# An early-fusion layer in one kernel: the mask of the transposed scores moves into spare rows of the shift product, the image comes on 96 partitions, the sink values lie in PSUM

## The chip, the cores and the metric

The kernel runs on one core of a Trainium2 chip. The metric is the device time of one execution in microseconds (us). The profile is of one execution; its span runs from the first to the last recorded instruction.

## The reference, cut to what matters

64 images of 12 x 224 x 224 become 196 tokens each, 32 text tokens join them (T = 228), then come an attention layer with 12 heads of 16 and a mixture of 8 experts. Everything is fp32.

```python
pooled = x.reshape(Bb, Cc, n, K, n, K).sum(axis=(3, 5))     # 16 x 16 patches, n = 14
h = jnp.einsum('bcij,ce->bije', pooled, channel_weights)    # 12 channels -> 192
h = concat([h, txt]); xn = layernorm(h)
...
att = jnp.einsum('bhqd,bhkd->bhqk', rope(q), rope(k)) * scale
att = jnp.where(causal, att, -inf)
att = softmax(concat([sink, att]))[..., 1:]                 # one sink value per head
h = h + ((att @ v) @ W_proj + b_proj) * rezero
h = h + moe(layernorm(h))                                   # top 2 of 8 experts
```

## The kernel before, in words

The first pass is a software pipeline over the 64 images. One step works on five images at once: p (loaded, pooled, channels summed), a (first norm, q, k and v, rotation, turns), m (scores and their row maxima), t (scores again, transposed, with the maximum taken off, then exp and attend) and z (projection, second norm, gate, slots). Every engine runs its own list of these pieces in an order written by hand (step_tensor, step_scalar, step_vector, pass1_gpsimd), and semaphores join the lists. The second pass runs the experts over the scattered rows; nothing in it is edited.

The order of TensorE in a step, with S for score_t, C for score and T for turn_qk: S0 C0, project, S1 C1 S2 C2, turn_xn, S3, attend 0, make_qk 0, C3 S4, turn_xf, make_qk 1, C4 S5, gate_logits, C5 S6, attend 1, S7 C6, rank, S8 C7 C8, attend 2, T0 T1 T2, turn_shift, make_v, turn_y, T3 T4 T5, sum_channels, turn_yn. S2, S5 and S8 are the ones that treat the second half of the keys for four heads; the other six S treat the first half (and the sink row) for two heads.

The pieces that the change and the prediction touch:

- The image. load_image (L406) is one transfer: 112 partitions (4 channels of a group x 14 patch rows x 2 halves) times 3 groups, each piece 8 image rows in one run. fold_image (L686, GpSimd) adds the two halves of a group, 896 elements; pool_image (L502, VectorE) sums it to 14 values; spread_patches (L694, GpSimd) multiplies them with a 0/1 table so that each patch row stands in its own columns; sum_channels (L844, TensorE) multiplies by the channel weights, three groups for each of two halves of the tokens.
- The transposed scores. score_t (L953 to L964) adds three products in PSUM: k times q, `sel` times shift_t (takes off the row maximum), and the identity times mask_k (the causal mask, L956 and L959). shift_t has 128 rows of which 26 are in use.
- The shift. max_scores (L571, VectorE) leaves the row maxima in `top`; make_shift (L578) takes the larger of `top` and the sink value; turn_shift (L939, TensorE) turns it, waiting also for `routed`, which assign sets (`slot`, L675); round_shift (L795, ScalarE) rounds it to the high part; split_shift (L586, VectorE) makes the low part and shift_ready, on which S0 of the next step and turn_xf wait.
- The rotation. rotate (L533, L535, VectorE) reads make_qk's result, add_rotation (L719, GpSimd) adds, high_parts (L747, ScalarE) and low_parts (L726, GpSimd) split q and k into pieces for turn_qk (L906). exp_gap (L833, ScalarE) waits for choose (L620, VectorE), exps are L805 and L808; place_q is L548, copy_y L814, weigh L644 to L657, place_k L559, normalize L593 to L598, turn_yn L1003, copy_yn L820, norm2_apply L770 (it waits for scattered rows, L1284).

VectorE's order in the middle of a step is: rotate 0, max 3, pool_image 1, rotate 1, max 4, max 5, choose, max 6, pool_image 2, max 7, max 8, make_shift, assign, place_k 1, split_shift, weigh, place_k 3, normalize, place_k 5. GpSimd's is: first statistics, fold 0, second statistics, fold 1, add_rotation 0, fold 2, add_rotation 1, low_parts 0 and 1, spread_patches, scatters.

## Time and profile before

| | |
|---|---|
| median of 3 runs | 2945.84 us (2934.99 to 2946.96) |
| the profiled execution | 2942.38 us, of which the span is 2940.6 us |
| TensorE, busy share of the span | 95% |
| GpSimd / VectorE / ScalarE, busy share | 69% / 70% / 58% |
| mean granted TensorE clock | 0.983 of full speed |
| first pass / second pass | until about 1730 us / the rest |

The shares of busy time are means over both passes. Matmuls are pipelined and the records show each with its latency, so a busy TensorE isn't one at its peak; the spacing of starts tells what one matmul costs. A wait in brackets at a row of the timeline is the idle time of the engine in front of it, with the instruction that ended it.

### The profile page before, as it was taken

The numbers are of one execution on the slowest core, as the hardware profiler recorded it, in microseconds if no ns is written. First come the engines' busy times: TensorE is split into PE (matmuls) and PEld (weight loads), VectorE is DVE, ScalarE is ACT, GpSimd is POOL, SyncE is SP. The second block draws the span as 40 slices with busy tenths as digits, with TensorE's granted clock in tenths as the row PEclk, the third lists the DMA queues.
The fourth block names the chain that finished last, engine by engine and source line by source line (L and its number), as shares of the span: only waits on it lengthen the run. The fifth ranks groups of instructions, "written<-read, shape, count | busy, mean of one in ns | idle before, by whom it ended". The sixth has DMA issues, their size and how long they took to land. (4 is left out here: it accounts for less than half of the span.)

```text
span 2940.6 us, 65980 instructions
## 1 busy us (share of the span) xinstructions
PE 2788.6 (95%) x21712; PEld 2515.0 (86%) x21712; DVE 2049.6 (70%) x5657; ACT 1692.5 (58%) x4074; POOL 2022.5 (69%) x2070
## 2 busy tenths in 40 slices
PE   2899999999999999999999976999999999999998
PEld 1788888888888888888888866999999989999997
DVE  3577777777777777777777745767676767676766
ACT  1466666666665666666566644655565656565655
POOL 3578888888888888788888733655566555565655
PEclk9899999999999999999999988999999999999999
DMA  6455455544443444444344222333333333323242
GB/s 191 141 176 175 167 165 173 156 122 122 115 107 106 119 121 122 119 111 111 107 121 121 56 48 61 56 60 51 63 55 65 49 65 49 65 45 65 46 68 43
DMA packets 206006, 292.47 MB, mean 99 GB/s; under 512 B 95670, under 2 KB 167675, under 8 KB 205874
## 3 DMA queue, kind: packets, MB, share of 16 engines
q1 hardware_dynamic: 82642, 241.41, 28.2%
q0 software_dynamic: 122880, 47.00, 11.4%
q10 hardware_dynamic: 352, 2.41, 0.3%
q8 instruction: 69, 1.13, 0.2%
q14 instruction: 63, 0.52, 0.1%
HBM read 201.73 MB, written 93.90 MB: 101 GB/s over the span
## 5 line engine op out<-in xcount | busy, mean ns | idle before, releaser
L1493 POOL DMA_INDIRECT out<-arena,who x320 | 595.3, 1860 | 291.4 <-DVE who L1372 180.5
L571 DVE TENSOR_REDUCE top<-bank 114x2 f32<-114x456 f32 (+1 forms) x576 | 352.8, 622 | 87.3 <-PE bank L930 71.1
L686 POOL TENSOR_TENSOR arena<-arena 112x896 f32<-112x896 f32 x192 | 403.0, 2100 | 13.2 <-DMA arena<-in_x 13.2
L1466 PE MATMUL bank<-w_dn,hid 128*114 128x192 f32 x3840 | 401.9, 264 | 0.0
L1466 PEld LDWEIGHTS bank<-w_dn,hid 128*114 128x114 f32 x3840 | 390.3, 180 | 0.0
L1439 ACT ACTIVATE arena<-bank 128x456 f32<-128x456 f32 x320 | 176.3, 551 | 342.1 <-PE bank L1430 332.2
L1284 POOL DMA_INDIRECT moe_rows<-row,slot x256 | 294.4, 1150 | 103.9 <-issue 85.0
L548 ACT ACTIVATE pieces<-bank 64x456 fp32r<-64x456 f32 x384 | 209.4, 545 | 147.1 <-PE bank L906 144.9
L1443 DVE TENSOR_TENSOR arena<-bank,arena 128x456 f32<-128x456 f32 x320 | 201.5, 630 | 96.6 <-ACT arena L1439 84.6
L726 POOL TENSOR_TENSOR qk<-rot_c,qk 114x384 fp32r<-114x384 f32 x256 | 253.8, 1013 | 19.0 <-ACT qk L747 19.0
L1426 PE MATMUL bank<-pieces 128*128 128x456 f32 x640 | 241.2, 377 | 21.9 <-DVE arena L1443 15.2
L805 ACT ACTIVATE prob<-bank 115x456 f32<-115x456 f32 x384 | 208.0, 542 | 78.0 <-PE bank L956 77.3
L1430 PE MATMUL bank<-pieces 128*128 128x456 f32 x640 | 238.5, 373 | 0.0
L1455 DVE TENSOR_TENSOR hid<-arena,hid 128x456 fp32r<-128x456 f32 x320 | 201.6, 630 | 52.3 <-ACT hid L1450 34.3
L1429 PE MATMUL bank<-pieces 128*128 128x456 f32 x640 | 237.9, 372 | 0.0
L1450 ACT ACTIVATE hid<-arena 128x456 fp32r<-128x456 f32 x320 | 186.9, 584 | 88.1 <-DVE arena L1443 86.7
L1428 PE MATMUL bank<-pieces 128*128 128x456 f32 x640 | 237.5, 371 | 0.0
L1427 PE MATMUL bank<-pieces 128*128 128x456 f32 x640 | 236.8, 370 | 0.0
L1483 POOL TENSOR_TENSOR rms<-rms,minus_half 114x4 f32<-114x4 f32 x82 | 85.4, 1042 | 193.5 <-DVE rms L1364 193.5
L906 PE MATMUL bank<-ident_r,qk 114*128 114x114 f32 x1536 | 202.1, 282 | 10.7 <-POOL qk L726 10.7
L502 DVE TENSOR_REDUCE pooled<-arena 112x14 f32<-112x896 f32 x192 | 206.5, 1076 | 6.4 <-POOL arena L686 6.4
L906 PEld LDWEIGHTS bank<-ident_r,qk 114*128 114x128 f32 x1536 | 186.5, 196 | 23.0 <-POOL qk L726 23.0
(171 smaller groups left out, 7216.3 us busy)
## 6 DMA issues: line engine op xcount, KB each, us to landing
arena<-in_x SPq DMA_DIRECT2D x63, 2352.0 KB, 11.8
arena<-moe_rows SPq DMA_DIRECT2D x82, 363.4 KB
moe_rows<-filler SPq DMA_DIRECT2D x20, 1453.5 KB
out<-h SPq DMA_DIRECT2D x64, 171.0 KB
out<-arena,who POOLq DMA_INDIRECT x320, 5.0
arena<-in_w_t SPq DMA_DIRECT2D x9, 512.0 KB
arena<-in_w_t SPq DMA_DIRECT2D x18, 256.0 KB
moe_rows<-row,slot POOLq DMA_INDIRECT x256, 7.3
```

The lines of the kernel that those rows point to most:

```text
L571: nc.vector.tensor_reduce(dst, src, AX.X, ALU.max).then_inc(maxed[k], 1)
L686: nc.gpsimd.tensor_tensor(xin[at.par][:, g, 0:mid], xin[at.par][:, g, 0:mid], xin[at.par][:, g, mid:XF], ALU.add).then_inc(x_folded, 1)
L726: ins = nc.gpsimd.tensor_tensor(lo, of, first.bitcast(fp32), ALU.subtract)
L906: ins = nc.tensor.matmul(dst[:, TT * (2 * pair + half):TT * (2 * pair + half + 1)], src, ident_r[0:TT, 0:TT], start=True, stop=True)
L1284: nc.gpsimd.indirect_dma_start(out=moe_rows[0:SLOTS, :], out_offset=bass.IndirectOffsetOnAxis(ap=slot[at.par][:, 2 * t + k:2 * t + k + 1], ...
L1426: nc.tensor.matmul(dst, hi[:, 0, col], za_hi[:, :], start=True, stop=False)
L1427: nc.tensor.matmul(dst, hi[:, 0, col], za_lo[:, :], start=False, stop=False)
L1428: nc.tensor.matmul(dst, lo[:, 0, col], za_hi[:, :], start=False, stop=False)
L1429: nc.tensor.matmul(dst, hi[:, 1, col], zb[:, :], start=False, stop=False)
L1430: ins = nc.tensor.matmul(dst, lo[:, 1, col], zb[:, :], start=False, stop=True)
L1466: ins = nc.tensor.matmul(dst, hid2[:, j, h_part, at], w_dn2[e_par][:, j, w_part, :], start=(j == 0 and s % 2 == 0 and part == 0), stop=(j ...
L1493: nc.gpsimd.indirect_dma_start(out=out[:, :], out_offset=bass.IndirectOffsetOnAxis(ap=who[par][:, s:s + 1], axis=0), in_=ys[par][:, s, :], ...
```

## The change

Three parts. The mask of the transposed scores goes into rows 14 to 127 of shift_t, which are written once (`low`), and `sel` gets the identity in these rows, so that the product that takes off the maximum adds the mask as well. For that the heads are taken in two groups of six: the shift has 14 rows (TOP) per group and is turned in four pieces instead of two. The image comes on 96 partitions (8 row pairs x 12 channels) in eight transfers with runs of 448 elements; it is folded and pooled in three bands of 5, 5 and 4 patch rows, the spread is left out, and sum_channels is one product for each half of the tokens. The sink values of make_shift lie in PSUM columns. In the lists of VectorE and GpSimd some pieces change place.

```diff
-XP = GRP * SIDE * 2
-XF = HALF * IMG
+XP = CH * HALF
+XF = 2 * IMG
+BANDS = ((0, 5), (5, 10), (10, SIDE))
+NG = len(BANDS)
+TOP = 2 * PAIRS + 2
...
-        sel[h, h] = -1
-        sel[HEADS + h, h] = -1
+        sel[h % PAIRS, h] = -1
+        sel[PAIRS + h % PAIRS, h] = -1
+        sel[TOP + q, h, q] = 1
+    low = np.zeros((128, 3, TT), f)
+    low[TOP:, 0] = low[TOP:, 2] = later.T
...
+        sink_top = bank[7][0:TT, 480:480 + 2 * HEADS].rearrange("p (t a) -> p t a", t=2)
-        shift = sb("shift", [TT, 2, 128])
-        shift_hi = sb("shift_hi", [128, T], fp32r)
-        shift_t = sb("shift_t", [128, T], fp32r)
+        shift = sb("shift", [TT, 2, 2, TOP])
+        shift_hi = sb("shift_hi", [TOP, 2, 2, TT], fp32r)
+        shift_t = sb("shift_t", [128, 2, 3, TT], fp32r)
...
-            sp.dma_start(xin[at.par][:, :, :], x_img[at.b, :, :, :]).then_inc(x_loaded[at.par], 16)
+            for r in range(HALF):
+                sp.dma_start(xin[at.par][CH * r:CH * (r + 1), :, :], x_img[at.b, r, :, :, :]).then_inc(x_loaded[at.par], 16)
...
         def pool_image(dve, at, g):
-                wait(dve, x_spread, at.b - 1)
+                wait(dve, h_summed, at.b - 1)
+            lo, hi = BANDS[g]
             ins = nc.vector.tensor_reduce(
-                pooled[at.par][:, g, :],
-                xin[at.par][:, g, 0:XF // 2].rearrange("p (r j c) -> p j r c", r=HALF // 2, c=PATCH), AX.XY, ALU.add)
+                pooled[at.par][:, SIDE * lo:SIDE * hi],
+                xin[at.par][:, lo:hi, 0:IMG].rearrange("p i (j c) -> p i j c", c=PATCH), AX.X, ALU.add)
...
         def split_shift(dve, at):
-            nc.vector.scalar_tensor_tensor(out=shift_t[:, :], in0=shift_hi[:, :].bitcast(fp32), scalar=split[:, 2:3],
-                                           in1=bank[7][:, 0:T], op0=ALU.mult, op1=ALU.add).then_inc(shift_ready, 1)
+            turned = bank[7][0:TOP, 0:4 * TT].rearrange("p (g t n) -> p g t n", g=2, t=2)
+            for to, of in ((slice(0, 2), slice(0, 2)), (slice(2, 3), slice(1, 2))):
+                ins = nc.vector.scalar_tensor_tensor(out=shift_t[0:TOP, :, to, :], in0=shift_hi[:, :, of, :].bitcast(fp32),
+                                                     scalar=split[0:TOP, 2:3], in1=turned[:, :, of, :], op0=ALU.mult, op1=ALU.add)
+            ins.then_inc(shift_ready, 1)
...
         def fold_image(pool, at, g):
-            nc.gpsimd.tensor_tensor(xin[at.par][:, g, 0:mid], xin[at.par][:, g, 0:mid], xin[at.par][:, g, mid:XF],
+            nc.gpsimd.tensor_tensor(xin[at.par][:, lo:hi, 0:IMG], xin[at.par][:, lo:hi, 0:IMG], xin[at.par][:, lo:hi, IMG:XF],
...
-        def spread_patches(pool, at):
...
         def sum_channels(pe, at):
             for t, (lo, hi) in enumerate(((0, TT), (TT, SIDE * SIDE))):
-                for g in range(NG):
-                    ins = nc.tensor.matmul(bank[6][0:hi - lo, D * t:D * (t + 1)], spread[:, g, lo:hi], chan[:, g, :],
-                                           start=(g == 0), stop=(g == NG - 1))
+                ins = nc.tensor.matmul(bank[6][0:hi - lo, D * t:D * (t + 1)], pooled[at.par][:, lo:hi], chan[:, :],
+                                       start=True, stop=True)
...
         def turn_shift(pe, at):
-            for t in range(2):
-                ins = nc.tensor.transpose(bank[7][:, TT * t:TT * (t + 1)], shift[:, t, :], ident[0:TT, 0:TT])
+            for g in range(2):
+                for t in range(2):
+                    ins = nc.tensor.transpose(bank[7][0:TOP, TT * (2 * g + t):TT * (2 * g + t + 1)], shift[:, t, g, :],
+                                              ident[0:TT, 0:TT])
...
         def score_t(pe, a, m, t, k):
-                ins = nc.tensor.matmul(dst[0:TT, 0:2 * T].rearrange("p (a n) -> p a n", a=2)[:, :, 0:TT], ident_r[0:TT, 0:TT],
-                                       mask_k[:, 0:2, :], start=False, stop=True)
...
-                nc.tensor.matmul(dst[0:TT, 0:4 * TT], ident_r[0:TT, 0:TT], mask_k[:, :, :], start=True, stop=False)
...
         def step_vector(dve, p, a, m, t, z):
             maxima("6")
-            if p:
-                pool_image(dve, p, 2)
+            if z:
+                assign(dve, z)
             maxima("7 8")
             if m:
                 make_shift(dve, m)
-            if z:
-                assign(dve, z)
             if a:
                 place_k(dve, a, 1)
+            if p:
+                pool_image(dve, p, 2)
             if m:
                 split_shift(dve, m)
...
                 if a:
                     add_rotation(pool, a, 0)
-                if p:
-                    fold_image(pool, p, 2)
-                if a:
                     add_rotation(pool, a, 1)
                     low_parts(pool, a, 0)
                     low_parts(pool, a, 1)
                 if p:
-                    spread_patches(pool, p)
+                    fold_image(pool, p, 2)
```

## Rows read from the trace of the kernel before

**Rows 1.** The page's first part: busy time of each engine.

```profile
PE 2788.6 (95%) x21712; PEld 2515.0 (86%) x21712; DVE 2049.6 (70%) x5657; ACT 1692.5 (58%) x4074; POOL 2022.5 (69%) x2070
```

**Rows 2.** Windows of the first pass: busy us by engine, clock, DMA share.

```profile
700.00:1000.00 300.00, 296.59 (x2532) 261.34 (x2531) 223.21 (x670) 182.88 (x406) 242.39 (x302) 1.00 0.43 116
...
1700.00:1710.00 10.00, 8.66 (x79) 8.07 (x79) 6.96 (x27) 6.31 (x13) 8.01 (x8) 1.00 0.18 49
```

**Rows 3.** The line of copy_yn from 400 to 1600 us: ns min/median/max.

```profile
L820 ACT ACTIVATE yn_t<-bank x46: 546/547/548, 421.1 to 1580.3; 97x456 f32<-97x456 f32 x46
```

**Rows 4.** Timeline of one step, front half: start, length, engine, line.

```profile
806.99 0.45 PE L953 MATMUL bank<-pieces 128*115 128x456 f32 x1
...
813.80 2.09 POOL L686 TENSOR_TENSOR arena<-arena 112x896 f32<-112x896 f32 x1
...
816.87 1.07 DVE L502 TENSOR_REDUCE pooled<-arena 112x14 f32<-112x896 f32 x1
...
820.39 0.63 DVE L571 TENSOR_REDUCE top<-bank 114x2 f32<-114x456 f32 x1 [0.71 <-PE bank L930]
...
821.21 0.48 ACT L833 ACTIVATE gexp<-best 114x1 f32<-114x1 f32 x2 [1.44 <-DVE best L620]
...
823.03 1.98 POOL L726 TENSOR_TENSOR qk<-rot_c,qk 114x384 fp32r<-114x384 f32 x2 [0.29 <-ACT qk L747]
...
825.26 1.55 PE L906 MATMUL bank<-ident_r,qk 114*128 114x114 f32 x12
```

**Rows 5.** Timeline of the same step, back half, up to the next score_t.

```profile
827.76 0.37 ACT L795 ACTIVATE shift_hi<-bank 128x228 fp32r<-128x228 f32 x1
...
828.16 0.45 DVE L586 SCALAR_TENSOR_TENSOR shift_t<-shift_hi,split,bank 128x228 fp32r<-128x228 f32 x1 [0.56 <-ACT shift_hi L795]
...
830.59 2.16 PE L844 MATMUL bank<-chan,spread 112*114 112x192 f32 x12
...
832.59 0.56 PE L1003 MATMUL bank<-ident,yn 114*97 114x114 f32 x4
...
832.91 0.45 PE L953 MATMUL bank<-pieces 128*115 128x456 f32 x1
```

**Rows 6.** Timeline of the step after the last image: no sum_channels.

```profile
1701.44 1.55 PE L906 MATMUL bank<-ident_r,qk 114*128 114x114 f32 x12
...
1707.79 0.63 PE L1003 MATMUL bank<-ident,yn 114*97 114x114 f32 x4 [1.30 <-DVE yn L598]
1708.19 0.44 PE L953 MATMUL bank<-pieces 128*115 128x456 f32 x1
```

**Rows 7.** Waits, 400 to 1600 us: us in total, times, longest.

```profile
PE bank L939 <- DVE slot L675: 9.2, 28, 0.4
```

**Rows 8.** Timeline of TensorE: a mask matmul and the start behind it.

```profile
807.49 0.27 PE L956 MATMUL bank<-mask_k,ident_r 114*114 114x228 f32 x1
...
807.60 0.36 PE L919 MATMUL bank<-mask_q,ident_r 114*114 114x456 f32 x1
```

**Rows 9.** Groups by shape, whole span: busy us, mean ns, idle before.

```profile
L686 POOL TENSOR_TENSOR arena<-arena 112x896 f32<-112x896 f32 x192 | 403.0, 2100 | 13.2 <-DMA arena<-in_x 13.2
...
L694 POOL TENSOR_TENSOR spread<-pooled,patch 112x196 f32<-112x196 f32 x192 | 96.0, 527 | 18.8 <-DVE pooled L502 18.8
...
L502 DVE TENSOR_REDUCE pooled<-arena 112x14 f32<-112x896 f32 x192 | 206.5, 1076 | 6.4 <-POOL arena L686 6.4
...
L571 DVE TENSOR_REDUCE top<-bank 114x2 f32<-114x456 f32 x384 | 234.9, 626 | 71.1 <-PE bank L930 71.1
```

**Rows 10.** The line of make_shift from 400 to 1600 us: ns min/median/max.

```profile
L578 DVE TENSOR_TENSOR shift<-top,sink_tok x47: 208/589/614, 413.3 to 1598.4; 114x48 f32<-114x48 f32 x47
```

**Rows 11.** Transfers: KB and us to landing; one issue in SP's timeline.

```profile
arena<-in_x SPq DMA_DIRECT2D x63, 2352.0 KB, 11.8
...
moe_rows<-row,slot POOLq DMA_INDIRECT x256, 7.3
```

```profile
824.49 0.32 SPq L406 DMA_DIRECT2D arena<-in_x  x1
```

More of the change, by code:

```diff
@@ L67, in constants @@
     split[:, 1] = np.where(term >= 2, -1, 0)
-    split[HEADS:2 * HEADS, 2] = -1
-    split[2 * HEADS + 1, 3] = -1
+    split[PAIRS:2 * PAIRS, 2] = -1
+    split[2 * PAIRS + 1, 3] = -1
     small = np.zeros((128, 2 * E + 2), f)
@@ L78, in constants @@
             filler[:, par, s, COL_ID] = tokens + (par * T + 2 * q + s) % ROWS
-    rows = np.arange(XP)
     return {
@@ L84, in constants @@
         "mask_q0": np.ascontiguousarray(np.repeat(later[:, None], 4, 1)),
-        "mask_k": np.ascontiguousarray(np.repeat(later.T[:, None], 4, 1)),
+        "low": low,
         "sel": sel,
@@ L89, in constants @@
         "before": (q[:, None] < q[None, :]).astype(f),
-        "patch": ((rows[:, None] // 2) % SIDE == np.arange(SIDE)[None]).astype(f),
         "filler": filler,
     }
-CONST_NAMES = ["cos", "sin", "ident", "mask_q0", "mask_k", "sel", "split", "small",
-               "before", "patch", "filler"]
+CONST_NAMES = ["cos", "sin", "ident", "mask_q0", "low", "sel", "split", "small",
+               "before", "filler"]
 class Batch:
@@ L179, in build @@
         gate = sb("gate", [C, 2, E])
-        arena = sb("arena", [128, 2 * NG * XF])
-        xin = [arena[0:XP, NG * XF * i:NG * XF * (i + 1)].rearrange("p (g f) -> p g f", g=NG) for i in range(2)]
-        pooled = [sb(f"pooled{i}", [XP, NG, SIDE]) for i in range(2)]
-        spread = sb("spread", [XP, NG, SIDE * SIDE])
+        arena = sb("arena", [128, 2 * SIDE * XF])
+        xin = [arena[0:XP, SIDE * XF * i:SIDE * XF * (i + 1)].rearrange("p (i f) -> p i f", i=SIDE) for i in range(2)]
+        pooled = [sb(f"pooled{i}", [XP, SIDE * SIDE]) for i in range(2)]
         h = [sb(f"h{i}", [TT, 2, D]) for i in range(2)]
@@ L209, in build @@
         top = sb("top", [TT, 2, HEADS])
-        shift = sb("shift", [TT, 2, 128])
-        shift_hi = sb("shift_hi", [128, T], fp32r)
-        shift_t = sb("shift_t", [128, T], fp32r)
+        shift = sb("shift", [TT, 2, 2, TOP])
+        shift_hi = sb("shift_hi", [TOP, 2, 2, TT], fp32r)
+        shift_t = sb("shift_t", [128, 2, 3, TT], fp32r)
         prob = sb("prob", [128, HEADS * T])
         staging, start = {}, 0
-        for name, rows, width in (("mask_q0", TT, 4 * TT), ("mask_k", TT, 4 * TT), ("sel", 128, HEADS * (TT + 1)),
+        for name, rows, width in (("mask_q0", TT, 4 * TT), ("low", 128, 3 * TT), ("sel", 128, HEADS * (TT + 1)),
                                   ("before", TT, TT), ("sink_col", 128, HEADS)):
@@ L371, in setup_sync @@
                     sp.dma_start(dst, src).then_inc(loaded, 16)
-            for g in range(NG):
-                sp.dma_start(chan[:, g, :], chan_w[GRP * g:GRP * (g + 1), :].unsqueeze(1)
-                             .to_broadcast([GRP, SIDE * 2, D])).then_inc(loaded, 16)
-            for name in ("mask_q0", "mask_k", "sel", "before"):
+            sp.dma_start(chan[:, :], chan_w.unsqueeze(0).to_broadcast([HALF, CH, D])).then_inc(loaded, 16)
+            for name in ("mask_q0", "low", "sel", "before"):
                 src = const[name]
@@ L442, in setup_vector @@
             dve.wait_ge(step0, n)
-            for tile in (xn[:, :, :, C:C1], yn[:, :, :, C:C1], shift[:, :, 2 * HEADS:2 * HEADS + 2],
+            for tile in (xn[:, :, :, C:C1], yn[:, :, :, C:C1], shift[:, :, :, 2 * PAIRS:TOP],
                          val[0][:, :, :, HD:HD + 1], val[1][:, :, :, HD:HD + 1]):
@@ L682, in fold_image @@
         def fold_image(pool, at, g):
-            pool.wait_ge(x_loaded[at.par], 16 * (at.half + 1))
-            mid = XF // 2
-            nc.gpsimd.tensor_tensor(xin[at.par][:, g, 0:mid], xin[at.par][:, g, 0:mid], xin[at.par][:, g, mid:XF],
+            pool.wait_ge(x_loaded[at.par], 16 * HALF * (at.half + 1))
+            lo, hi = BANDS[g]
+            nc.gpsimd.tensor_tensor(xin[at.par][:, lo:hi, 0:IMG], xin[at.par][:, lo:hi, 0:IMG], xin[at.par][:, lo:hi, IMG:XF],
                                     ALU.add).then_inc(x_folded, 1)
-        def spread_patches(pool, at):
-            wait(pool, h_summed, at.b)
-            for g in range(NG):
-                pool.wait_ge(x_pooled, NG * at.b + g + 1)
-                ins = nc.gpsimd.tensor_tensor(spread[:, g, :].rearrange("p (i j) -> p i j", j=SIDE),
-                                              pooled[at.par][:, g, :].unsqueeze(1).to_broadcast([XP, SIDE, SIDE]),
-                                              patch[:, :].unsqueeze(2).to_broadcast([XP, SIDE, SIDE]), ALU.mult)
-            ins.then_inc(x_spread, 1)
         def inverse_std(pool, at, norm):
```

52 lines of the change are left out of this document (26 added, 26 removed).

## The prediction, on record before the changed kernel ran

> **What bounds the kernel now.** I read the page first: TensorE is busy 95% of the span, GpSimd 69%, VectorE 70% [rows 1]. Then the windows: from 100 to 1700 us the first pass repeats one step per image, and in 300 us of it TensorE is busy 296.59 us, GpSimd 242.39, VectorE 223.21 [rows 2]. The second pass isn't edited. copy_yn runs once a step, 46 times from 421.1 to 1580.3 us [rows 3]: a step takes 1159.2 / 45 = 25.76 us.
>
> A busy TensorE suggests that work taken from it comes back in full. The timeline says otherwise. I follow one step from its first score_t matmul (806.99) to the next (832.91), and give times as "step time", less 806.99. TensorE finds two short gaps: at 18.27 the turns of q and k (T0) start just after GpSimd's last low parts (ended 823.03 + 1.98, step time 18.02) [rows 4], and the turn of the shift waits for `slot` in 28 of 46 steps [rows 7]. So a second chain runs only some tenths behind TensorE. Its front half: make_qk, rotate on VectorE, the max of score 5 (13.40), choose, exp_gap on ScalarE (14.22), exp 6, high_parts 1, low_parts 1 on GpSimd (16.04), T0 (18.27) [rows 4]. Its back half: place_q, copy_y, round_shift (20.77), split_shift on VectorE (21.17), weigh, place_k, normalize, turn_yn (25.60), the next score_t (25.92) [rows 5]. The trace holds an experiment on it: the last step without sum_channels. There TensorE stands 1.30 us, until yn is normalized, and turn_yn comes 1707.79 - 1701.44 = 6.35 us after T0, the next score_t 6.75 us after it [rows 6]. In the ordinary step that is 832.91 - 825.26 = 7.65. Taking away sum_channels, 2.16 us long, gave 0.9: the chain took the rest.
>
> **TensorE's share of the change.** A mask matmul of 228 columns costs the spacing to the next start, 807.60 - 807.49 = 0.11 us [rows 8]; one of 456 columns I take at twice that less a little, 0.2. Six and three of them go: 1.3 us a step. Sum_channels is 12 instructions in 2.16 us [rows 5], so (2.16 - 0.33) / 11 = 0.166 each; eight go: 1.3 us. Two transposes of the shift become four; two stand in 0.39 us with the pipe's latency, so two more cost 0.1 each: +0.2. Net -2.4 us. TensorE alone could make a step in about 25.76 - 0.4 (its gaps) - 2.4 = 23.0.
>
> **GpSimd.** Fold: 896 elements take 2100 ns, and the spread's 196 take 527 [rows 9], so 2.25 ns an element. The new bands (1120, 1120, 896) cost 2.61 + 2.61 + 2.10 = 7.32 against 6.31; the three spreads (1.58) go. Net -0.6, GpSimd isn't the bound. The order matters more: the third fold moves from in front of add_rotation 1 to behind low_parts 1. In the front half add_rotation 1 is thus free of it, and the band's sum is late instead (below).
>
> **VectorE.** The reduce of 896 takes 1076 ns, of 456 626, so 1.02 ns an element: 1120 cost 1.31, +0.23 for each of two bands [rows 9]. The same width of input to split_shift: 228 elements take 0.45 [rows 5]; 456 add 0.24, 0.69, and a second instruction of 228 follows with 0.45 less the overlap of some 0.08. Bounds: 456 elements at least 0.62, the reduce's time, no overlap at most: +0.6 (0.5 to 0.7) on the back half. round_shift from 228 to 456 columns goes from 367 to the 547 ns of copy_yn, +0.18, also there [rows 3, 5]. Make_shift has minimum 208 and median 589 ns [rows 10]: it is short where GpSimd's spread doesn't run beside it. The spread goes anyway; with the sink in PSUM it should stay near 0.21. It is worth 0.4 us, but not on the chain: T0 to T2 end later.
>
> **Front half, new.** Up to score 5, TensorE sheds four short and two long masks, 0.44 + 0.4 = 0.8 us. What could keep the chain from following: pool_image 1 stands in front of rotate 1 and now needs a fold of 2.61. Fold 1 starts at 6.81 now [rows 4]. In front of it on GpSimd stand the statistics of the new image, which I estimate 0.6 us earlier since sum_channels ends early, and fold 0, 0.5 longer: it starts at 6.7 and ends at 9.3. Pool_image 1 started at 9.88 and would come with TensorE's lead so far, 0.5, at 9.4; with 1.31 it ends at 10.7. Rotate 1 and max 4 take 820.39 - 0.71 - 816.87 - 1.07 = 1.74 from there to the start of the wait for score 5 [rows 4]: 12.4, and max 5 is due at 12.6, so it isn't held, by 0.2. exp_gap and all behind it come 0.8 earlier: low_parts 1 ends at 17.2, T0 at 17.47. TensorE itself, with 0.2 more shed in S6 and S7 and 0.2 in S8, would be there at about 17.0 and waits some 0.4.
>
> **Back half, new.** From T0 to the next score_t: 6.75 of the step without sum_channels, + 0.18, + 0.6 = 7.53. Sum_channels, now 0.8 us long, fits into TensorE's wait. Assign has left the way of turn_shift. New in front of split_shift: pool_image 2, a new wait of VectorE for GpSimd; behind it in VectorE's list stand split_shift, weigh, place_k 3 and normalize, for which turn_yn, S0 and turn_xf wait. The third fold (2.10) starts when low_parts 1 ends, 17.2, and ends at 19.3; the reduce (1.08) ends at 20.4. round_shift ends at 17.47 + 2.90 + 0.18 = 20.55, so split_shift isn't held, with only 0.1 us to spare. The scatters, last on GpSimd, end at 25.0, statistics ask for it at 26.
>
> Step: 17.47 + 7.53 = 25.0; for the tie in front of split_shift I take 25.05. Saving 0.71 us; 60 steps have all stages: -43 us. The steps of filling and draining (eight) both lose masks and gain the longer split; setup has two small loads fewer: 0, bounds -5 and +5. The profiled execution took 2942.38 us (span 2940.6), 0.1% under the median of the runs, 2945.84: forecast 2900.
>
> **The image's transfer.** One transfer of 336 pieces of 7168 bytes becomes eight, 1344 pieces of 1792 bytes, each over 12 partitions. SP spends 0.32 us on one issue [rows 11], so 2.6 for eight; behind them stand store_h2 and load_text, which are asked for some us later. The image is issued at 17.5 of a step (20.5 in future) and folded two steps on at 3 to 5: 33 us, and it lands in 11.8 [rows 11]. Below nothing: small pieces may let the scatters in between, too little here to count, since the chain above doesn't pass through them. Above nothing: the landing would have to grow from 11.8 to more than 30 us before a fold waits for it.
>
> **Rivals.**
> (a) TensorE sets the pace after all, 23.0 us a step: 2942 - 2.7 x 60 = 2780. For it stands the busy share; against it the 1.30 us of [rows 6]. 5%.
> (b) The front half doesn't move: the longer fold 1 or the norm chain holds rotate 1 by 0.8 us, and the back half takes what is left: 18.27 + 7.53 = 25.8, so 2942. GpSimd and VectorE meet at 9.3 and 9.4, so half a microsecond that I overlooked is half of this. 17%.
> (c) Slower: the third band, pooled in front of split_shift. It decides as soon as low_parts 1, fold and reduce end more than 0.8 us behind round_shift (0.1 to spare, 0.7 of gain); where the fold stretches by 1.5 us, the step is 26.4 and the kernel 2981. The order speaks for it, the durations of [rows 9], the same to a few ns in each step, against it. 7%.
> (d) The transfer spread over fewer engines: if the image takes a third longer (15.7 us, 18.3 with the issues) it is still hidden, but the scatters, 7.3 us from issue to landing [rows 11], share the engines. A third more for them, 2.4 us, could hold norm2_apply, which waits for them. If its slack is half of that, 1.2 us a step come back: 2900 + 72 = 2972. Against it: the chain doesn't pass through norm2_apply today. 5%.
> The rows show an image over 112 partitions landing in 11.8 us, and none over 12. 
> (e) TensorE's clock: it will stand 1.2 us once a step. In the window of the 1.30 us gap the granted clock is 1.00, 2.4 GHz [rows 2], which speaks against it. Half clock for 3 us a step would cost 1.5 x 60 = 90, 2990. 3%.
>
> **Chances.** The forecast (2875 to 2915) 63%; the rivals as above. A measurement here can tell about 0.5%, 15 us. Faster by more: forecast, (a) and the upper part of (b), 72%; within 15%; slower 13%. The range reaches from 2865, beyond the best of my bounds (front 0.1 and split 0.1 better, 12 us), to 2946, which takes in (b).
>
> **What the profile should show.** No mask matmuls in score_t, 4 instructions in sum_channels; a wait of turn_yn for `yn` of about 1 us in each step, the sign that the chain sets the pace; copy_yn every 25.05 us; T0 17.5 us into the step, still waiting for low_parts; split_shift ending 0.6 us later after its start; make_shift at 0.21; no fold waiting for its image. Wrong would be: pool_image 2 waiting for its fold with split_shift right behind it (c), rotate 1 waiting on pool_image 1 (b), no wait before turn_yn (a), norm2_apply waiting for scatters every step (d), slow stretches of matmuls in mid-pass (e).

## The result, and the profile after

The changed kernel takes 3500.73 us (median of 4 runs, 3475.61 to 3502.59) against 2944.28 us beside it: ratio 1.1881, 95% interval 1.1836 to 1.1927. It is 556 us slower where 46 us less were forecast, far outside the stated range of 2865 to 2946, and on the other side.

The page of the changed kernel: the head, the slices of clock and transfers, and two of its costliest groups, the fold and the first statistics of a new image.

```profile
span 3500.8 us, 64984 instructions
## 1 busy us (share of the span) xinstructions
PE 2944.9 (84%) x20752; PEld 2584.5 (74%) x20752; DVE 2105.8 (60%) x5722; ACT 1712.6 (49%) x4074; POOL 1982.6 (57%) x1878
...
PEclk9888778787887878888878889879999999999999
DMA  6777677767676667766766767114333333333333
```

```profile
L689 POOL TENSOR_TENSOR arena<-arena 96x1120 f32<-96x1120 f32 (+1 forms) x192 | 462.0, 2407 | 37.6 <-DMA arena<-in_x 37.6
...
L515 DVE BATCH_NORM_STATS2 st<-h 114x6 f32<-114x192 f32 x256 | 79.1, 351 | 279.2 <-DMA h<-in_txt 247.2
```

The first reading is the clock line: from slice 2 to slice 24 the granted clock is 0.7 to 0.8 of full speed, where it was 1.00 in the windows of before [rows 2]. The second is the line under it. Transfers keep the DMA engines busy for 6 to 7 tenths of the time in the same slices, but they moved no more for it. The windows say it with numbers; the columns are busy us of each engine, then the granted clock, the DMA share and GB/s:

```profile
700.00:1000.00 300.00, 231.10 (x1697) 193.03 (x1698) 166.02 (x491) 132.36 (x289) 169.87 (x195) 0.82 0.71 106
```

Before, this window had a DMA share of 0.43 at 116 GB/s [rows 2]. Now 0.71 of the engines' time moves 106. The engines are held 1.65 times as long for less. What waits for it? Not the fold: its wait for `in_x`, 37.6 us in all, is one wait at the start. Two other things wait.

Up to about 900 us it is the text. In this part SyncE also issues a block of filler rows (`moe_rows<-filler`, the last at 813 us) in each step. VectorE's first statistics (L515) stand until the text tokens of the new image have landed: 21 times, 247.2 us in all, nearly all of it in this part. SyncE's issue of the text, one instruction of 0.34 us at most before, takes up to 16.63 us here, behind the eight of the image. SyncE's and VectorE's timeline:

```profile
442.37 16.63 SPq L410 DMA_DIRECT2D h<-in_txt  x1
```

```profile
472.18 0.62 DVE L515 BATCH_NORM_STATS2 st<-h 114x6 f32<-114x192 f32 x2 [16.60 <-DMA h<-in_txt]
```

From 900 us on it is the scatters: norm2_apply (L763) waits for them 30 times, 145.4 us in all. The timeline of ScalarE and TensorE over one long step of this part and the start of the next:

```profile
1089.99 0.55 ACT L814 ACTIVATE yn_t<-bank 97x456 f32<-97x456 f32 x1 [1.66 <-PE bank L999]
1102.52 0.98 ACT L763 ACTIVATE row<-h,shifted,rstd 114x192 f32<-114x192 f32 x2 [5.31 <-DMA moe_rows<-row,slot]
1129.47 0.55 ACT L814 ACTIVATE yn_t<-bank 97x456 f32<-97x456 f32 x1 [0.42 <-PE bank L999]
```

```profile
1088.97 0.98 PE L999 MATMUL bank<-ident,yn 114*97 114x114 f32 x4 [1.22 <-DVE yn L601]
1091.58 1.98 PE L1007 MATMUL bank<-w_out,yn_t 97*114 97x192 f32 x8
1103.56 0.99 PE L1017 MATMUL bank<-ident,row 114*96 114x114 f32 x4 [4.00 <-ACT row L763]
```

norm2_apply (L763) stands 5.31 us until the scatters of the image before the last have landed, and turn_xf (L1017) stands 4.00 us behind it. From there TensorE runs at half clock:

```profile
1093.00:1102.00 9.00, 6.56 (x56) 5.26 (x54) 6.49 (x12) 2.22 (x5) 6.49 (x8) 1.00 0.82 110
1104.00:1108.00 4.00, 4.00 (x14) 2.69 (x12) 0.85 (x2) 1.78 (x4) 0.00 (x0) 0.50 0.81 101
1108.00:1112.00 4.00, 4.00 (x23) 3.62 (x25) 1.56 (x6) 0.72 (x2) 3.05 (x4) 0.50 0.75 92
1112.00:1120.00 8.00, 8.00 (x61) 6.52 (x53) 3.79 (x17) 2.71 (x8) 5.84 (x5) 0.50 0.12 27
```

0.50 is 1.2 GHz, and TensorE is busy all the time in those windows. This step, from copy_yn (L814) to copy_yn, takes 1129.47 - 1089.99 = 39.5 us; the one before it, with no wait for scatters, 25.2 us (1064.80 to 1089.99). The two alternate from about 1050 to 1280 us, and around that steps from 25 to 40 us are mixed; up to 900 us all steps are 33.8 to 44.9 us. The changed kernel is 44 us behind at the first copy_yn (180.87 us against 136.80), 299 at the 19th (899.45 against 600.79) and 554 at the last of the first pass (2302.10 against 1748.20). So nearly all of the loss is in the first pass, and more than half of it comes before norm2_apply waits for the first time. The step of the forecast, 25.05 us, is there wherever nothing disturbs it; the transfers disturb most of them.

SyncE's own queue shows the other side. An issue took 0.32 us before [rows 11]; the eight of an image now take 0.95 us each at best:

```profile
1020.65 7.57 SPq L405 DMA_DIRECT2D arena<-in_x  x8
1028.62 0.29 SPq L420 DMA_DIRECT2D out<-h  x1
```

### The profile page after: what moved, and what is told of

Its sections match the earlier page's. It is cut to its first block and busy times, and to the rows that moved or that the text cites. A ratio compares the mean times of both kernels' runs of the same rounds, so it can differ in the third digit from the quotient of the medians.

```text
span 3500.8 us, 64984 instructions
## 1 busy us (share of the span) xinstructions
PE 2944.9 (84%) x20752; PEld 2584.5 (74%) x20752; DVE 2105.8 (60%) x5722; ACT 1712.6 (49%) x4074; POOL 1982.6 (57%) x1878
## 3 DMA queue, kind: packets, MB, share of 16 engines
q10 hardware_dynamic: 1440, 2.41, 0.5%
## 5 line engine op out<-in xcount | busy, mean ns | idle before, releaser
L689 POOL TENSOR_TENSOR arena<-arena 96x1120 f32<-96x1120 f32 (+1 forms) x192 | 462.0, 2407 | 37.6 <-DMA arena<-in_x 37.6
L712 POOL TENSOR_TENSOR rot_c<-rot_c,rot_s 114x192 f32<-114x192 f32 x256 | 145.2, 588 | 309.4 <-DVE rot_s L535 309.4
L698 POOL TENSOR_TENSOR var<-mv,ln_eps 114x2 f32<-114x2 f32 x128 | 25.1, 196 | 475.5 <-DVE mv L519 475.5
L855 PE MATMUL bank<-w_qkv,xn_t 97*114 97x384 f32 x512 | 255.8, 634 | 5.0 <-DVE rot_s L535 2.3
L502 DVE TENSOR_REDUCE pooled<-arena 96x70 f32<-96x1120 f32 (+1 forms) x192 | 236.2, 1231 | 36.9 <-POOL arena L689 36.8
L912 PE MATMUL bank<-mask_q,ident_r 114*114 114x456 f32 x192 | 88.0, 458 | 191.4 <-DVE top L571 191.4
L515 DVE BATCH_NORM_STATS2 st<-h 114x6 f32<-114x192 f32 x256 | 79.1, 351 | 279.2 <-DMA h<-in_txt 247.2
```

The source lines that it names most:

```text
L689: nc.gpsimd.tensor_tensor(xin[at.par][:, lo:hi, 0:IMG], xin[at.par][:, lo:hi, 0:IMG], xin[at.par][:, lo:hi, IMG:XF], ALU.add).then_inc(x_f ...
L855: ins = nc.tensor.matmul(bank[6][0:TT, 0:2 * D], xn_t[:, c, TT * t:TT * (t + 1)], w_qkv[:, c, 0:2 * D], start=(c == 0), stop=(c == 1))
```

## The experiments

They ask three things: what makes the transfer slow (e1, e5, e6), what the computing side is worth (e2 to e4), and what holds it once the transfer is quick (e7 to e15).

### e1: the transfer by itself

A kernel with nothing but loads: seven forms, three images each, one after the other; a memset marks the end of each form.

> No computation: only three images loaded in each of seven forms, one form after the other, a small VectorE memset marking when each form has landed; the output is not filled. Theory N (narrow destination: eight transfers of 12 neighbouring partitions, in which all engines write to the same few partitions at a time): form 2, the changed kernel's, takes about 26 us an image as in its trace (1344 pieces of 233 ns over 12 engines), form 6 (same 12 partitions at a time, but long runs of source) is as slow, while form 3 (same pieces of 1792 bytes, but 96 partitions in each transfer) and form 5 (1792-byte pieces over 112 partitions) take 8 to 13 us like form 1. Rival S (small pieces): forms 2, 3, 4 and 5 are all slow, about 24 us, form 6 is fast. Rival E (12 engines instead of 16): forms 2, 3 and 6 alike at 16/12 of form 1, so 12 to 15 us, and form 4 (8 engines) slower still.

Timeline of VectorE; the wait in brackets is what three images took:

```profile
30.56 0.07 DVE L93 MEMSET mark<- 128x8 f32 x1 [30.56 <-DMA wide<-in_x]
108.52 0.07 DVE L93 MEMSET mark<- 128x8 f32 x1 [77.89 <-DMA wide<-in_x]
145.82 0.07 DVE L93 MEMSET mark<- 128x8 f32 x1 [37.24 <-DMA wide<-in_x]
187.62 0.07 DVE L93 MEMSET mark<- 128x8 f32 x1 [41.73 <-DMA wide<-in_x]
218.58 0.07 DVE L93 MEMSET mark<- 128x8 f32 x1 [30.90 <-DMA gaps<-in_x]
296.16 0.07 DVE L93 MEMSET mark<- 128x8 f32 x1 [77.51 <-DMA wide<-in_x]
331.34 0.07 DVE L93 MEMSET mark<- 128x8 f32 x1 [35.12 <-DMA wide<-in_x]
```

| form of an image's load | us an image |
|---|---|
| one transfer, 112 partitions, 7168-byte pieces (before) | 9.9 |
| eight transfers of 12 neighbouring partitions, 1792-byte pieces (after) | 26.0 |
| 14 transfers (one for each patch row) over 96 partitions, channels outermost | 12.4 |
| the same, row pairs outermost | 13.9 |
| three transfers of 112 partitions, 1792-byte pieces | 10.3 |
| eight transfers of 12 neighbouring partitions, one run of 25088 bytes in each partition | 25.8 |
| one transfer, 96 partitions, one run of 25088 bytes in each | 11.7 |

The second and sixth rows settle it: with runs of 1792 or of 25088 bytes, 12 neighbouring partitions take 26 us; small pieces on 112 partitions cost 0.4. Rival (d) took 12 engines for 16, which would be a factor of 1.33. With 12 channels outermost and a wide destination the run shows 12.4 against 10.3, a factor of 1.2, and with 8 row pairs outermost 1.35. The narrow destination is another factor of two. The Trainium skill has a rule for it (SBUF — State Buffer, Door 1: The DMA port swizzle): the rate goes by how many of 16 ports a single transfer's partitions reach, four neighbouring partitions share one, and 16 ports give 436 GB/s. By that 12 neighbours reach three, 82 GB/s, an estimate of 29 us for 2.41 MB if one transfer ran at a time. The run shows 2.41 MB / 26.0 us = 93 GB/s, so it agrees to 12%. The 243 GB/s of the wide load (9.9 us) is well below 436, so by this rule the ports aren't what bounds that one. No form here has 12 partitions that lie apart; the runs show that a narrow block of neighbours is slow, not that ports are the reason.

### e5 and e6: the same two forms of load in the kernel before

In e5 only the load is edited, in e6 as well, the one narrow, the other wide with as many issues:

```diff
-            sp.dma_start(xin[at.par][:, :, :], x_img[at.b, :, :, :])
+            for r in range(8):   # e5
+                sp.dma_start(xin[at.par][14 * r:14 * (r + 1), :, :], x_img[at.b, 14 * r:14 * (r + 1), :, :])
+            for r in range(8):   # e6
+                sp.dma_start(xin[at.par][:, :, IMG * r:IMG * (r + 1)], x_img[at.b, :, :, IMG * r:IMG * (r + 1)])
```

> The kernel before, with its image loaded in eight transfers of 14 neighbouring partitions (7168-byte pieces) in place of one over 112; nothing else is edited. Theory N (a transfer to a few neighbouring partitions is slow, whatever its pieces): the transfers by themselves took 26 us an image against 9.9, the bands of the scatters meet them, norm2_apply waits for scattered rows, TensorE falls to half clock behind it, and the kernel goes the way of the changed one: 3250 to 3500 us. Theory S (the small pieces or the new layout of the computing did it): 2944 us, within 0.5%.

> The kernel before, with its image loaded in eight transfers, each over all 112 partitions with one image row of each piece (896 bytes, 2688 pieces an image); nothing else is edited. It has the issues of the change and still smaller pieces, without the narrow destination. Theory N: the transfer stays hidden, 2944 us within 0.5%. Theory I (many issues in SyncE's queue near the end of a step hold back what TensorE reports of sum_channels): sum_channels is reported 1 us or more after its last matmul in most steps, TensorE stands in front of the projection, and the kernel takes 3000 to 3100 us. Theory S (small pieces cost): over 3000 us with norm2_apply waiting for rows.

e5: 3651.59 us, ratio 1.2386 (1.2358 to 1.2414). e6: 2953.76 us, 1.002 (1.001 to 1.003). The windows of 1000 to 1300 us in e5 and 700 to 1000 us in e6, and, from 700 to 1600 us, a group of e5's waits (us in total, times, longest):

```profile
1000.00:1300.00 300.00, 224.11 (x1757) 192.84 (x1755) 154.69 (x468) 124.84 (x280) 170.97 (x212) 0.87 0.58 80
```

```profile
ACT row L771 <- DMA moe_rows<-row,slot: 206.4, 21, 11.4
```

```profile
700.00:1000.00 300.00, 296.43 (x2529) 261.34 (x2530) 222.78 (x670) 182.37 (x407) 241.45 (x300) 1.00 0.47 118
```

The narrow load alone, with 7168-byte pieces and none of the change's computing, makes the kernel before slower than the changed one, and more than was expected. Both waits of the changed kernel are in it, for text (18 times, 179 us) and for scatters (42 times, 415 us). Eight issues and 896-byte pieces cost 6 us in all. Shown: a narrow destination by itself is enough for a loss of this size.

### e2: the change with a wide load

14 transfers, one for each patch row, over all 96 partitions; partitions are ordered by channel first, and the channel weights are laid out to match. The computing is that of the changed kernel.

```diff
-            for r in range(HALF):
-                sp.dma_start(xin[at.par][CH * r:CH * (r + 1), :, :], x_img[at.b, r, :, :, :])
+            for i in range(SIDE):
+                sp.dma_start(xin[at.par][:, i, :], x_img[at.b, i, :, :, :])
```

> The changed kernel with the image in 14 transfers, each one patch row over all 96 partitions (partition = 8 times channel + row pair), same pieces of 1792 bytes, same computation. Theory N: the transfer is hidden again, a step takes about 25.1 us, the kernel 2900 us, 17% faster than the changed one. Rival S (small pieces): no better than the changed kernel, 3450 to 3550 us. Rival C (the computing side of the change is slow by itself): 3400 to 3550 us as well, but with fast packets in the trace. SP issues 14 transfers in some 13 us, which might delay store and text a little.

3158.09 us, ratio 1.0711 (1.0692 to 1.0730), where 2900 was expected. The waits for text and scatters are gone, and 343 us with them, but the steps are 28.0 to 31.3 us, not 25.05. ScalarE and TensorE at one boundary of steps:

```profile
1034.31 0.33 ACT L748 ACTIVATE h<-bank 114x192 f32<-114x192 f32 x1 [3.31 <-remote]
1034.75 0.55 ACT L814 ACTIVATE yn_t<-bank 97x456 f32<-97x456 f32 x1
```

```profile
1030.14 0.86 PE L837 MATMUL bank<-chan,pooled 96*114 96x192 f32 x4
1032.22 0.63 PE L999 MATMUL bank<-ident,yn 114*97 114x114 f32 x4 [1.22 <-issue]
1035.35 2.90 PE L1007 MATMUL bank<-w_out,yn_t 97*114 97x192 f32 x8 [1.51 <-ACT yn_t L814]
```

sum_channels (L837) ends at 1031.00, and copy_h (L748), which waits for nothing else, starts at 1034.31. The trace's record of the semaphore says why: TensorE's report of the sum (the raising of the semaphore that others wait for) came at 1034.29. copy_yn stands behind copy_h in ScalarE's list, the projection waits for copy_yn, and then TensorE's eight matmuls of the projection take 2.90 us instead of the 1.56 that they take at full clock in e7: half clock.

### e3: nearly no load at all

From the third image on only 2 of 14 patch rows are loaded; the rest of the image is that of an earlier one.

> The changed kernel, which from the third image on loads only 2 of the 14 patch rows (the other rows keep old values, so that the output is that of other images); all computation and all transfers' count stay. If the transfer's bytes are what the change loses to (N, S or E), a step takes 25.0 to 25.2 us as in the prediction's chain and the kernel 2890 to 2910 us. If the computing side is slow by itself (rival C), or the eight issues of SP are (0.95 us each in the changed kernel's trace), it stays near 3500 us.

3004.05 us, ratio 1.0192 (1.0166 to 1.0217), granted clock 0.96; 2890 to 2910 us was expected. So even with a DMA share of 0.13 the changed kernel isn't faster than before: the bytes of the transfer aren't all that it loses to. This isn't yet the computing by itself: the eight issues are still made, and the report of the sum (explained at e2) is late in every step from 400 to 1600 us, by up to 2.2 us.

### e4: the mask and the sink values alone

The kernel before, its image and all orders as they were, with the mask in spare rows and the sink values in PSUM.

> The kernel before with the mask in spare rows and the sink in PSUM alone; image, spread and all orders as before. TensorE sheds 1.3 us of masks and gains 0.2 for the turns. By the chain: T0 comes 0.5 to 0.8 us earlier, the back half gains 0.18 + 0.6 for rounding and splitting, less what was slack in front of turn_yn (0.6): a step of 25.2 to 25.8 us, kernel 2905 to 2945. If TensorE sets the pace, as its busy share says: 25.76 - 1.1 - 0.4 = 24.3 us, 2855.

2906.16 us, ratio 0.9846 (0.9824 to 0.9869). Steps of 24.8 to 25.1 us from 560 us on (up to 25.5 in front of that); TensorE stands nowhere, and the clock is 1.00:

```profile
1000.00:1300.00 300.00, 298.44 (x2553) 257.98 (x2552) 233.60 (x712) 190.22 (x423) 251.47 (x313) 1.00 0.44 119
```

This is the gain that the forecast had for the whole change. The image part in its wide form adds nothing to it: e7 and e9 below are slower, and with normalize moved e10 and e11 are level.

### e7 and e8: two ways to cure the wide load

e7: as e2, with SyncE waiting for copy_h of the image before the last, so that its 14 issues lie behind sum_channels. e8: as e2, with each matmul of sum_channels made three times (1.3 us, same result), to fill the gap in front of turn_yn.

```diff
             wait(sp, x_pooled, NG * (at.b - 1))
+            wait(sp, h_copied, at.b - 1)        # e7
```

> The changed kernel with 14 transfers over 96 partitions, as in the run before of that kind (3158 us), but SyncE starts to issue them only after copy_h of the image before the last, so behind sum_channels and not across it. Theory I: the 3.3 us between the last matmul of sum_channels and copy_h go, the clock stays at 1.00 for most of the first pass, steps of 25.1 us: 2860 to 2910 us. Theory C (TensorE's shorter work alone lets the clock fall, whenever the transfers are issued): steps stay at 28 to 31 us, 3120 to 3160. A middle, if the issues hold back another engine's report elsewhere in the step: 2950 to 3100, with a wait of over 1 us at another instruction.

> The changed kernel with 14 transfers over 96 partitions, issued as in the run of 3158 us, with each of the two matmuls of sum_channels made three times (1.3 us of TensorE in the gap in front of turn_yn; the result is the same). Theory I: the report of sum_channels still comes 1 to 3 us late, so the wait of the projection stays, and the kernel stays over 3050 us. Theory C (standing 1.2 us in front of turn_yn is what brings the half clock): the wait in front of turn_yn is under 0.3 us, the clock stays at 1.00, 2870 to 2930 us.

e7: 2958.45 us, 1.0034 (1.0017 to 1.0052). e8: 3033.47 us, 1.0285 (1.026 to 1.0309). Both lie outside what theories I and C gave; e7 lies in the range that was left for a wait elsewhere. In e8 the report of the sum still comes 2.1 us late (median of 43) and the steps are 26.7 us in the median, so the filler alone doesn't cure it. e7's report of the sum comes 0.01 us after the matmul in most steps, 0.6 in 15 of 46. Of its 50 steps from 300 to 1600 us, 29 are of 24.9 to 25.2, and 21 of 26.4 to 29.9. Windows in a good stretch, behind the 1.22 us that TensorE stands in front of turn_yn, and later in that step:

```profile
1034.00:1058.00 24.00, 23.58 (x204) 20.17 (x204) 19.03 (x55) 15.56 (x34) 19.68 (x23) 1.00 0.43 122
1060.00:1069.00 9.00, 9.00 (x40) 8.70 (x39) 3.68 (x11) 3.07 (x6) 6.54 (x10) 0.50 0.60 176
1072.00:1086.00 14.00, 13.85 (x129) 11.94 (x128) 11.67 (x33) 9.19 (x21) 10.02 (x11) 1.00 0.15 44
```

The gap is there in every step, the half clock behind it in two of five.

### e9: e7 with the gap filled

> The run with 14 transfers over 96 partitions issued behind copy_h (2958 us: 25.0 us in a good step, 27.8 to 29.8 us in the steps in which half clock follows the 1.22 us that TensorE stands in front of turn_yn), with each of the two matmuls of sum_channels made three times, so that TensorE has work in that gap; the result is the same. Theory C (the stand brings the half clock, and the half clock is all that is left over the steps of 25.0): wait in front of turn_yn under 0.3 us, granted clock 1.00 from 400 to 1600 us, steps of 25.0 to 25.2, 2900 to 2915 us. Theory D (the transfers or the layout bring the long steps, and the clock is only beside them): long steps stay, 2945 us or more.

2918.25 us, 0.9893 (0.9868 to 0.9918), just above the 2900 to 2915 expected. The clock is 1.00 in each window from 400 to 1600 us, and all 51 steps are 25.4 to 25.5 us: the filler costs 0.45 us a step and gives back the 1.24 that e7's steps have over 25.0 in the mean. Work that nobody needs makes the kernel 40 us faster. Theory C is shown for what was left in e7: with the gap filled and everything else the same, the half clock is gone.

### e10, e11, e12, e13: the chain shortened, and a step that doesn't follow

If split_shift, weigh, place_k 3 and normalize set the step, normalize in front of weigh and place_k 3 should shorten it. e10 does that to e7, e11 to e4; e12 moves weigh behind place_k 5 as well; e13 is e12 with SyncE's issues behind norm1_apply, in the middle of the step.

```diff
+            if t:
+                normalize(dve, t, 0)
+                normalize(dve, t, 1)
             if z:
                 weigh(dve, z)
             if a:
                 place_k(dve, a, 3)
-            if t:
-                normalize(dve, t, 0)
-                normalize(dve, t, 1)
```

> The same run of 2958 us with one edit in VectorE's list: normalize comes in front of weigh and place_k 3, not behind them, so yn is ready about 1.5 us sooner. If the chain through split_shift, weigh and normalize sets the step, as forecast, turn_yn waits for nothing, TensorE has no gap there, the clock stays at 1.00, and the step falls until TensorE (23.7) or the front half (S0 to low_parts 1 to T0) holds it: 24.0 to 24.6 us, 2830 to 2880 us. If instead the scatters, now 1.4 us later, or place_k 3 hold the next step: no gain, 2900 to 2960.

> The kernel before with the mask part and the sink values alone (2906 us), with the same edit in VectorE's list. There TensorE has the 12 matmuls of sum_channels and stands nowhere over 0.1 us in a step of 24.95, so if TensorE and the chain are level in it, the edit can give 0.1 to 0.3 us a step at most: 2890 to 2906 us. If the chain alone held it, as much as in the run beside it, 2860.

> The run of 2904.7 us (14 transfers issued behind copy_h, normalize first) with weigh moved behind place_k 3 and 5 as well. In that run the step stayed at 25.0 us though turn_yn no longer waited: C0 waits 0.50 us (place_k 5 is the last on VectorE that it needs) and the projection 0.71 us, since copy_yn starts 1.0 us after turn_yn has ended, while SyncE is in its 14 issues. If both waits are ties of the chain: C0's 0.5 goes, the projection's stays: 24.4 to 24.6 us a step, 2868 to 2885 us. If the place of the issues is all that counts: no change, 2900 to 2908.

> The run beside it, with SyncE's 14 issues behind norm1_apply instead of behind copy_h: 4 to 18 us into a step, so that neither sum_channels nor turn_yn ends during them. Theory I (a run of issues holds back what another engine reports): the 1.0 us in front of copy_yn goes, the projection waits under 0.2 us, and TensorE alone or the front half sets a step of 23.8 to 24.2 us: 2835 to 2865 us, the fastest of all. Some other instruction in the middle of the step may show a wait named remote instead; if that one lies on the front half, 2870 to 2905.

| | median us | ratio | interval | steps from 300 to 1600 us, median |
|---|---|---|---|---|
| e10 | 2904.68 | 0.9855 | 0.9826 to 0.9883 | 25.0, four of 26.6 to 28.1 |
| e11 | 2898.29 | 0.9822 | 0.9789 to 0.9854 | 24.8 (25.0 to 25.5 up to 560 us) |
| e12 | 2909.51 | 0.9883 | 0.9861 to 0.9905 | 25.0, three of 26.6 to 28.1 |
| e13 | 2916.59 | 0.9909 | 0.9874 to 0.9944 | 25.0, three of 27.4 to 28.1 |

turn_yn waits no longer, so the clock stays up (0.99 in e10), but the step sticks at 25.0: the expectations of e10, e12 and e13, 2830 to 2885 us, missed, and only that of e11 (2890 to 2906) held. The wait has moved to copy_yn. e13, ScalarE:

```profile
1017.21 0.33 ACT L749 ACTIVATE h<-bank 114x192 f32<-114x192 f32 x1 [0.65 <-PE bank L838]
1017.43 0.32 ACT L750 ACTIVATE h<-bank 82x192 f32<-82x192 f32 x1
1018.72 0.55 ACT L815 ACTIVATE yn_t<-bank 97x456 f32<-97x456 f32 x1 [0.97 <-remote]
```

and TensorE, which has turned yn by 1016.96 and then stands for the projection:

```profile
1016.40 0.56 PE L1000 MATMUL bank<-ident,yn 114*97 114x114 f32 x4
...
1019.32 0.91 PE L1008 MATMUL bank<-w_out,yn_t 97*114 97x192 f32 x4 [1.38 <-ACT yn_t L815]
```

The semaphore events of the trace for the same stretch, beside GpSimd's scatters (all in us of the span; the ends of matmuls in a trace are modelled from their starts):

```
e13: report of   matmul ended   report came       scatters: start, end
T5 (L900)          1015.87       1016.41          1015.81, 1016.93
sum (L838)         1016.56       1017.18
yn (L1000)         1016.96       1018.70          1017.23, 1018.35
S0 (L952)          1017.38       1018.75
C0 (L916)          1017.95       1018.82
```

SyncE issued nothing here (it was idle from 1012.9 to 1022.6), so theory I, that SyncE's issues alone hold back what TensorE reports, has fallen. All 209 reports of TensorE that are seen over 0.3 us late in e13 from 400 to 1600 us came so beside one of GpSimd's scatters. Of VectorE and ScalarE no report is seen late, but 384 of VectorE's and 174 of ScalarE's are missing from this record, while none is missing from those of the kernel before, e14 and e15.

### e14 and e15: no scatters

e14 is e12, e15 is e2, without the scatters of the first pass and the waits for them: the rows of the mixture of experts are left out.

> The run of 2909.5 us (issues behind copy_h, normalize first, weigh last) without the scatters of the first pass: the rows of the mixture of experts are left out, all else is computed. In that run turn_yn's last matmul ended 1.7 us before its report, and the report came 0.35 us after GpSimd's fourth scatter; SyncE was idle there in the run beside it (2916.6 us) and the report was as late. Theory P (GpSimd's scatters hold back what TensorE reports): every report of TensorE comes 0.014 us after its matmul, the projection waits under 0.3 us, the step falls from 25.0 to 23.8 to 24.4 us, and the kernel is at 2830 to 2875 us. Theory F (the first pass is held at 25.0 by something else): 24.9 to 25.0 us, 2895 to 2910.

> The changed kernel with 14 transfers over 96 partitions, issued across sum_channels (3158 us), without the scatters of the first pass; the rows of the mixture of experts are left out. Theory P: with SyncE's issues where they were, the report of sum_channels comes 0.014 us after its last matmul, not 3.3 us, copy_h follows at once, steps are 25.1 us but for those in which half clock falls behind the gap in front of turn_yn: 2900 to 2990 us. Theory I (SyncE's issues alone hold it): the report stays 1 us or more late, over 3050 us.

e14: 2826.57 us, 0.9603 (0.9584 to 0.9621), a little below the range expected. e15: 2923.98 us, 0.993 (0.9907 to 0.9952). In neither does one report of TensorE or VectorE between 400 and 1600 us come over 0.3 us late. In e15 SyncE's issues cross sum_channels as in e2, and the report comes 0.014 us after it, not 3.3. Theory P is shown: without the scatters no report is held. Whether it is GpSimd's issuing of them or their transfers isn't separated, since both are gone in these runs. e14's steps are 24.3 and 24.7 us in turn, at full clock:

```profile
1000.00:1300.00 300.00, 289.00 (x2499) 250.44 (x2499) 243.12 (x722) 192.86 (x433) 190.63 (x229) 1.00 0.36 104
```

Of the 80 us between the spans of e12 and e14, 51 lie in the first pass (its last copy_yn comes at 1705.28 and 1654.49), 30 of them the 0.5 us a step; the other 29 lie in the second pass, which works on filler rows here. e15's first pass ends at 1755.57 and e7's at 1764.34: to take the scatters away does nearly the same as to move SyncE's issues, and both keep the gap in front of turn_yn and its half clock. The steps of e14, 24.5 us in the mean, missed the 24.4 at most that was expected by 0.1; in the front half turn_xn waits up to 1.09 us for xn.

## Why the prediction was wrong, step by step

**The step that failed** is the paragraph on the image's transfer: "Above nothing: the landing would have to grow from 11.8 to more than 30 us before a fold waits for it", and so nothing in the sum. The sentence itself held; behind the first image no fold waits. But the cost isn't paid there. By e1 the image needs 26 us of a 25 us step, and whatever else uses the same engines or stands behind it in SyncE's queue pays. That "behind them stand store_h2 and load_text, which are asked for some us later" was given no price either, and VectorE stood 247 us for the text. Rival (d) had one of the two places (norm2_apply, which waits for scatters: 145 us) and 5%, with a price from a third more time, where the run showed 2.6 times; no rival had the text. The rate was bounded by a row of another shape, "over 112 partitions landing in 11.8 us, and none over 12", and I took that as the value; as a bound from one side only, it should have widened the range. Undone (e2), it gives back 343 of the 556 us.

**The second failure** was to take the semaphore's report as free. In e2 reports of the sum that come up to 3.4 us late, and the half clock behind them, cost 200 us (e2 to e7): sum_channels now ends inside the scatters. In the kernel before it ends 0.14 or 0.6 us after the last of them, and no report was late; no row of it could show this.

**Rival (e)**, the clock: "It will stand 1.2 us once a step" was exact (1.22 us). That the clock holds was argued from one gap of 1.30 us at which it was 1.00 [rows 2, 6], one case. In e7 it fell behind 21 such gaps of 50, and these steps are 1.4 to 4.9 us longer, 2.8 to 3.4 in most. The price, 1.5 us in each of 60 steps, is near the mean of e7 (1.24), by luck: it was meant for every step. The chance, 3%, was too low. Filling the gap gives back 40 us net of the filler's own 0.45 us a step (e7 to e9).

**The chain.** Its own steps came out nearly to the tenth. In the undisturbed step of the changed kernel T0 comes 1081.87 - 1064.53 = 17.34 us after S0 (forecast 17.47), the step takes 25.2 (25.05), the two instructions of split_shift 1.04, the reduce of 1120 elements 1.30 (1.31), make_shift 0.20 (0.21). The reason given for the last was wrong: in the kernel before the short ones, 208 ns, also ran beside the spread, and in e4, which keeps the spread, all take 0.20 us. It is the sink in PSUM that did it.

The lines of VectorE in that step:

```profile
1082.07 0.20 DVE L578 TENSOR_TENSOR shift<-top,bank 114x48 f32<-114x48 f32 x1
...
1083.90 1.08 DVE L502 TENSOR_REDUCE pooled<-arena 96x56 f32<-96x896 f32 x1 [0.25 <-POOL arena L689]
1084.94 1.04 DVE L588 SCALAR_TENSOR_TENSOR shift_t<-shift_hi,split,bank 14x456 fp32r<-14x456 f32 x2
```

pool_image 2 waits 0.25 us for its fold, so rival (c)'s tie is there but doesn't decide. Rivals (a) and (b) did not happen. That the forecast's 2900 us is what the mask and sink part gives alone (2906) is in part luck: there TensorE, with all of sum_channels still in its list, is level with the chain.

**But was it the chain?** Only in part. In e4 it ties with TensorE, which stands nowhere at 24.95 us a step. In e10, e12 and e13 it ties with GpSimd's scatters and the reports behind them. Shortening the chain left the step at 25.0 until the scatters were gone too, and then it fell to 24.5. That a chain adds up to the step is no proof that it sets it.

**The fastest with the right result** is e11: the mask and the sink values alone, with normalize first, 2898.29 us, 1.8% under the kernel before; its interval overlaps those of e4 and e10. What stays open: why SyncE's issues of image and text take up to 16 us while filler rows are written, and why some reports beside a scatter are late and others aren't. In the kernel before reports at 1010.46 and 1010.91, inside a scatter from 1010.21 to 1011.34, came after 0.014 us. Nor is it shown what part SyncE's issues have. Alone they hold nothing (e15); without them the delay reaches 2.4 us (e13), with them 3.4 (e2); and e6, the kernel before with eight issues for one, has 114 late reports of turn_qk, up to 2.2 us, at no cost.

## What to carry to other kernels

Split a transfer by what lies along the free dimension and not by partitions: keep every transfer as many partitions wide as the tile, and where no row of the trace shows the new shape, measure it or leave its price open upward. Before costing a transfer at nothing, ask how much of the step it keeps the engines busy, who else sends and what stands behind it in its queue; slack of its own reader says nothing. Work taken off TensorE is a gain only if the chain gets shorter by as much; else it becomes a gap, and a gap can cost more than the work did.

## What the runs showed of the hardware

- A load into 12 neighbouring partitions moves 93 GB/s (26.0 us for 2.41 MB), into 112 partitions 243 GB/s (9.9 us), by run length nearly alike (12 partitions: 26.0 us with 1792 bytes, 25.8 with 25088; 112 partitions: 9.9 us with 7168 bytes, 10.3 with 1792).
- Eight or 14 such issues back to back take SyncE 0.95 and 0.99 us each, a lone one 0.32; eight over 112 partitions with 896-byte pieces 0.52. In the changed kernel up to 900 us single issues take up to 16.6 us.
- TensorE's reports can come up to 2.4 us late beside GpSimd's indirect scatters (e13), and up to 3.4 when SyncE issues too (e2); without scatters none is over 0.1 us late (e14, e15). Such a wait is named "remote" or "issue" in the timeline and not by its cause; it is seen by setting the end of the matmul beside the start of its reader.
- In e7 TensorE fell to 1.2 GHz, for 3 to 10 us at a time, behind 21 of 50 gaps of 1.22 us; with the gaps filled (e9) it stayed at 2.4 GHz.
